# Attention with a routed feed-forward: head values as column tiles, softmax sums over added probability tiles, and reciprocals spread by DMA

## The reference, cut to what matters

```python
def _L0_xattn_ref(q, k, v):              # q = layernorm(x), k = v = ctx; each (4, 512, 512)
    qh, kh, vh = (t.reshape(B, 8, 64, 512) for t in (q, k, v))
    qn, kn = _l2norm(qh, -2), _l2norm(kh, -2)         # over the 64 channels of a head
    sm = softmax(5.0 * einsum('bhdq,bhdk->bhqk', qn, kn), axis=-1)
    return einsum('bhqk,bhdk->bhdq', sm, vh).reshape(B, 512, 512)

x = x + _L0_xattn_ref(_layernorm(x), ctx, ctx)
x = x + _L0_ffn_ref(_layernorm(x), Wg, bg, W1, W2)    # top 2 of 4 experts, 512 tokens each
```

## Time and profile before

| what | us |
|---|---|
| median of 3 runs | 655.43 |
| the profiled execution, its own time | 656.28 |
| span of its trace | 654.3 |
| PE busy | 592.0 (90%) |
| DVE busy | 368.6 (56%) |
| ACT busy | 300.4 (46%) |
| POOL busy | 175.3 (27%) |
| reciprocals L762, mean of one | 3.35 |
| one half-unit's weighted values L1168 (8 records) in the chain | 3.44 to 3.55 |

### The profile page before, as it was taken

The page is one execution under the profiler, slowest core; times in us unless marked ns, Lnnn a source line. Parts: engine busy times, 40 slices in busy tenths (PEclk is TensorE's granted clock), DMA queues, the critical chain, the costliest instruction groups (busy, mean ns, idle before and its releaser), DMA issues.

```text
span 654.3 us, 8188 instructions
## 1 busy us (share of the span) xinstructions
PE 592.0 (90%) x2714; PEld 430.6 (66%) x2714; DVE 368.6 (56%) x638; ACT 300.4 (46%) x454; POOL 175.3 (27%) x139
## 2 busy tenths in 40 slices
PE   1899999999999951299999999999999999999994
PEld 1555555556555541168888888888888888888883
DVE  4678888888888878453425463434734245533312
ACT  2577776777678633044343332434333333434310
POOL 4544445445543600220021051040230120320002
PEclk9999999999999965579999999999999999999998
DMA  4423112221120023133333344151262332451001
GB/s 120 134 79 112 65 64 80 82 94 64 66 95 33 34 81 111 47 87 126 119 105 98 128 145 176 64 189 67 99 221 84 121 116 99 159 190 67 0 1 64
DMA packets 39636, 63.62 MB, mean 97 GB/s; under 512 B 3520, under 2 KB 20032, under 8 KB 39616
## 3 DMA queue, kind: packets, MB, share of 16 engines
q1 hardware_dynamic: 35776, 50.78, 22.7%
q0 software_dynamic: 3840, 12.59, 5.8%
HBM read 50.77 MB, written 12.58 MB: 97 GB/s over the span
## 4 chain that ended last, share of the span: by engine, by line
PE 73%; DVE 15%; issue 4%; POOL 1%; DMA 1%; DVEq 0%; ACT 0%; POOLq 0%
PE two L1299 28%; PE four L1329 9%; PE four L1328 9%; PE four L1326 9%; PE two L1168 9%; DVE p_inv L762 4%; PE four L1158 4%; PE bank_t L1185 1%; DVE o_norm L770 1%; PE bank_t L1137 1%; DVE junk L938 1%; PE bank_m L1145 1%; DVE x_all L772 1%; PE bank_t L1177 1%; DVE ss L723 1%
## 5 line engine op out<-in xcount | busy, mean ns | idle before, releaser
L677 ACT ACTIVATE h_f<-two 128x512 f32<-128x512 f32 x64 | 38.2, 598 | 231.7 <-PE two L1299 231.7
L1168 PE MATMUL two<-prob,v_t 128*128 128x512 f32 x256 | 116.7, 598 | 0.0
L1098 DVE TENSOR_TENSOR h_lo<-h_f,h_hi 128x512 fp32r<-128x512 f32 x64 | 44.1, 689 | 126.1 <-ACT h_hi L678 126.1
L1299 PE MATMUL two<-xt_hi,w_hi 128*128 (+1 forms) x256 | 103.0, 402 | 0.7 <-issue 0.7
L1299 PE MATMUL two<-xt_hi,w_lo 128*128 (+1 forms) x256 | 101.3, 396 | 0.0
L1299 PE MATMUL two<-xt_lo,w_hi 128*128 (+1 forms) x256 | 100.9, 397 | 0.0
L1329 PE MATMUL four<-w_hi,h_lo 128*128 128x512 f32 x256 | 100.5, 393 | 0.0
L1326 PE MATMUL four<-w_hi,h_hi 128*128 128x512 f32 x256 | 100.5, 392 | 0.0
L1328 PE MATMUL four<-w_lo,h_hi 128*128 128x512 f32 x256 | 100.4, 392 | 0.0
L1069 DVE TENSOR_TENSOR w_lo<-raw,w_hi 128x2048 fp32r<-128x2048 f32 x30 | 68.7, 2291 | 23.3 <-ACT w_hi L610 23.3
L582 ACT ACTIVATE prob<-four,rnorm 128x512 f32<-128x512 f32 x128 | 79.5, 695 | 2.3 <-PE four L1158 1.1
(11 more groups left out here) (167 smaller groups left out, 758.2 us busy)
## 6 DMA issues: line engine op xcount, KB each, us to landing
raw<-in_L_ffn_W SPq DMA_DIRECT2D x64, 512.0 KB, 3.9
x_all<-in_x SPq DMA_DIRECT2D x16, 256.0 KB, 2.7
c_sb<-in_ctx SPq DMA_DIRECT2D x16, 256.0 KB, 2.8
out<-x_all SPq DMA_DIRECT2D x16, 256.0 KB, 2.0
x2n_dram<-x2n SPq DMA_DIRECT2D x16, 256.0 KB, 2.1
cst<-in_consts SPq DMA_DIRECT2D x1, 354.5 KB, 4.8
x_got<-x2n_dram,idx_all POOLq DMA_INDIRECT x16
o_got<-out,idx_all POOLq DMA_INDIRECT x16
```

The source lines that it names most:

```text
L677: nc.scalar.activation(h_f[m % 2][:, :], z_ps[m % 2][:, :], ACT.Gelu)
L1098: nc.vector.tensor_tensor(h_lo[m % 2][:, :], h_f[m % 2][:, :], h_hi[m % 2][:, :].bitcast(F32), ALU.subtract).then_inc(h_split, 1)
L1168: last = nc.tensor.matmul(o_ps[h][:, :], v_t[u[1]][:, t, 2 * h:2 * h + 2, :] .rearrange("p a d -> p (a d)"), prob[h][t][:, :], start=(t == ...
L1299: return nc.tensor.matmul(z[:, :], w_part[c][:, w], x_k, start=start, stop=stop)
```

## The change

What it does:

- Values: the values of the two heads lie in one tile of 2 x 64 columns. Each head's matmul has 64 columns and writes its own half of the partitions of one PSUM bank (`o_ps[0]`), as a column tile. The ones leave this operand.
- Sums: probability tiles are added in pairs first (tile 0 + tile 1, tile 2 + tile 3), for head 0 on GpSimd and for head 1 on VectorE. Two matmuls per head with 64 columns of ones make the sums of it, again as column tiles, in `o_ps[1]`.
- Reciprocals: ACT copies the sums out (`take_sums`, one turn later). SP moves the row of each head into `few` (128 x 8), DVE inverts these 8 elements per partition, SP writes them to DRAM, waits, and reads them back broadcast to 64 partitions per head. `residual` waits for that read. For the last two units DVE inverts the full 128 x 512 tile, straight from PSUM.
- Order: on DVE `normalize_x2` of u-2 is now the first thing of a turn and `residual` and `statistics_x2` of u-1 are the last. On POOL the two additions are placed behind waits for `rq_ready` and `xsq_done`, and `key_remainders` moves to the end of the turn, behind a wait for `x2_done`. On PE `values` and `spread_queries` come ahead of the scores. ACT squares the keys and takes the values ahead of the exponentials. `first_low` is cut into 8 pieces of 128 x 512: three of them follow the sums of the last unit, the other five wait for `thr_done` of the router's search rounds, one each.

```diff
+FEW = 2 * D // P
+DVE_HEADS, POOL_HEADS = (1,), (0,)
...
+    inv_dram = nc.dram_tensor("inv_dram", (2 * D,), F32, kind="Internal").ap()
...
-            v_t = [att(f"v_t{n}", [P, TT, 4, DH]) for n in range(2)]
+            v_t = [att(f"v_t{n}", [P, TT, 2, DH]) for n in range(2)]
...
+            half_sum = [[att(f"half_sum{h}{n}", [P, D]) for n in range(2)] for h in range(2)]
+            few = att("few", [P, FEW])
+            few_inv = att("few_inv", [P, FEW])
...
+            def spread_inverse(u):
+
+                n = number(u)
+                sp.wait_ge(sum_taken, n + 1)
+                for h in range(2):
+                    half = slice(h * P // 2, (h + 1) * P // 2)
+                    sp.dma_start(few[half, :], p_sum[DH * h:DH * h + 1, :]).then_inc(few_in, 16)
+                sp.wait_ge(few_done, n + 1)
+                sp.dma_start(inv_dram.rearrange("(p j) -> p j", j=FEW), few_inv[:, :]).then_inc(few_out, 16)
+                sp.wait_ge(few_out, 16 * (n + 1))
+                for h in range(2):
+                    sp.dma_start(p_inv[DH * h:DH * (h + 1), :],
+                                 inv_dram[D * h:D * (h + 1)].rearrange("(a d) -> a d", a=1).broadcast_to([DH, D])
+                                 ).then_inc(inv_in, 16)
...
             load_next((2, 0))
+            spread_inverse((0, 0))
             store_unit((0, 0))
             end = UNITS // 2 - 1
             with sp.Fori(2, end) as h:
                 load_next((h, 1))
+                spread_inverse((h - 2, 1))
                 store_unit((h - 2, 1))
                 load_next((h + 1, 0))
+                spread_inverse((h - 1, 0))
                 store_unit((h - 1, 0))
             load_next((end, 1))
             for u in ((end - 2, 1), (end - 1, 0), (end - 1, 1), (end, 0), (end, 1)):
+                if number(u) < EARLY:
+                    spread_inverse(u)
...
+
+            def half_sums(u, n, h, reused):
+
+                pool.wait_ge(exp_done, TT * number(u) + 2 * n + 2)
+                if reused:
+                    pool.wait_ge(sums_ready, number(u))
+                nc.gpsimd.tensor_tensor(half_sum[h][n][:, :], prob[h][2 * n][:, :], prob[h][2 * n + 1][:, :],
+                                        ALU.add).then_inc(halves_done[h], 1)
...
-            def first_low(c):
+            def first_low(c, q):
 
                 pool.wait_ge(whi_done, c + 1)
-                nc.gpsimd.tensor_tensor(w_lo[c][:, :], raw[c][:, :], w_hi[c][:, :].bitcast(F32), ALU.subtract
-                                        ).then_inc(wlo_done, 1)
+                part = slice(q * HALF // 2, (q + 1) * HALF // 2)
+                low_part = nc.gpsimd.tensor_tensor(w_lo[c][:, part], raw[c][:, part], w_hi[c][:, part].bitcast(F32),
+                                                   ALU.subtract)
+                if q == 3:
+                    low_part.then_inc(wlo_done, 1)
...
             def unit(u, behind, ahead):
-                if not ahead:
-                    pool.wait_ge(x2n_done, number(u) - 1)
-                    for c in range(AHEAD):
-                        first_low(c)
+                n = number(u)
+                for h in POOL_HEADS:
+                    if ahead:
+                        pool.wait_ge(rq_ready, n + 2)
+                    half_sums(u, 0, h, behind > 0)
                 if ahead:
                     if behind:
 
-                        pool.wait_ge(exp_done, TT * number(u))
+                        pool.wait_ge(exp_done, TT * n)
                     key_norms(after(u))
+                for h in POOL_HEADS:
+                    if ahead > 1:
+                        pool.wait_ge(xsq_done, n + 3)
+                    half_sums(u, 1, h, behind > 0)
                 if ahead > 1:
+                    query_norms(after(after(u)))
+                if ahead > 2:
+                    prepare(after(after(after(u))))
+                if ahead > 1:
+                    if behind:
+                        pool.wait_ge(x2_done, n)
                     key_remainders(after(after(u)))
-                    query_norms(after(after(u)))
                 if behind:
                     finish(before(u))
-                if ahead > 2:
-                    prepare(after(after(after(u))))
 
...
+            pool.wait_ge(sums_ready, UNITS)
+            for q in range(3):
+                first_low(0, q)
             finish((UNITS // 2 - 1, 1))
+            for q in range(3, 8):
+                pool.wait_ge(thr_done, q - 1)
+                first_low(q // 4, q % 4)
...
@@ -578,6 +635,8 @@
                 act.wait_ge(scores_ready, g + 1)
                 if reused:
                     act.wait_ge(pv_done, g - TT + 1)
+                    for h in range(2):
+                        act.wait_ge(halves_done[h], 2 * (number(u) - 1) + t // 2 + 1)
...
-                nc.scalar.activation(p_sum[0:DH, :], o_ps[0][DH:P, :], ACT.Copy)
-                nc.scalar.activation(o_sb[0:DH, :], o_ps[0][0:DH, :], ACT.Copy).then_inc(o_taken[0], 1)
-                nc.scalar.activation(p_sum[DH:P, :], o_ps[1][0:DH, :], ACT.Copy).then_inc(sum_taken, 1)
-                nc.scalar.activation(o_sb[DH:P, :], o_ps[1][DH:P, :], ACT.Copy).then_inc(o_taken[1], 1)
+                nc.scalar.activation(o_sb[:, :], o_ps[0][:, :], ACT.Copy).then_inc(o_taken, 1)
+
+            def take_sums(u, reused):
+
+                n = number(u)
+                act.wait_ge(sums_ready, n + 1)
+                if reused:
+                    act.wait_ge(few_in, 32 * n)
+                nc.scalar.activation(p_sum[:, :], o_ps[1][:, :], ACT.Copy).then_inc(sum_taken, 1)
...
             def unit(u, behind, ahead):
+                if behind and ahead:
+                    take_sums(before(u), behind > 1)
+                if ahead:
+                    square_keys(after(u), behind + 1)
+                    take_v(after(u), behind + 1)
                 exponentials(u, 2, behind > 0)
-                if ahead:
-                    take_v(after(u), behind + 1)
                 exponentials(u, 3, behind > 0)
+                if ahead > 1:
+                    square_queries(after(after(u)), True)
                 if behind > 1:
                     take_x2t(before(before(u)))
-                if ahead > 1:
-                    square_queries(after(after(u)), True)
-                    round_keys(after(after(u)), True)
                 if ahead:
                     act.wait_ge(rk_done, number(u) + 2)
                     exponentials(after(u), 0, True)
                     exponentials(after(u), 1, True)
-                if ahead in (1, 2):
-                    split_hi(0, 2 - ahead)
+                if ahead > 1:
+                    round_keys(after(after(u)), True)
+                if not ahead:
+                    for c in range(AHEAD):
+                        split_hi(0, c)
                 take_o(u, behind > 0)
...
+            def invert_few(u):
+
+                n = number(u)
+                dve.wait_ge(few_in, 32 * (n + 1))
+                nc.vector.reciprocal(few_inv[:, :], few[:, :]).then_inc(few_done, 1)
+
             def invert_sums(u):
 
-                n = number(u)
-                dve.wait_ge(sum_taken, n + 1)
-                nc.vector.reciprocal(p_inv[:, :], p_sum[:, :]).then_inc(inv_done, 1)
-
-            def residual(u):
+                dve.wait_ge(sums_ready, number(u) + 1)
+                nc.vector.reciprocal(p_inv[:, :], o_ps[1][:, :]).then_inc(inv_done, 1)
+
+            def half_sums(u, n, h, reused):
+
+                dve.wait_ge(exp_done, TT * number(u) + 2 * n + 2)
+                if reused:
+                    dve.wait_ge(sums_ready, number(u))
+                nc.vector.tensor_tensor(half_sum[h][n][:, :], prob[h][2 * n][:, :], prob[h][2 * n + 1][:, :],
+                                        ALU.add).then_inc(halves_done[h], 1)
+
+            def residual(u, late=0):
 
                 n = number(u)
                 xu = x_all[:, bass.ds(n, 1), :].rearrange("p a d -> p (a d)")
-                dve.wait_ge(o_taken[1], n + 1)
-                dve.wait_ge(inv_done, n + 1)
+                dve.wait_ge(o_taken, n + 1)
+                if late:
+                    dve.wait_ge(inv_done, late)
+                else:
+                    dve.wait_ge(inv_in, 32 * (n + 1))
...
             def unit(u, behind, ahead):
+                if behind > 1:
+                    normalize_x2(before(before(u)), behind > 2)
+                if not ahead:
+                    invert_sums(before(u))
                 if ahead:
                     queries(after(u), after(after(u)) if ahead > 1 else None)
                     sum_key_squares(after(u))
-                if behind:
-                    invert_sums(before(u))
+                for h in DVE_HEADS:
+                    half_sums(u, 0, h, behind > 0)
+                if behind and ahead:
+                    invert_few(before(u))
                 if ahead > 1:
```

(76 more changed lines are left out.)

9 lines of the change are left out of this document (2 added, 7 removed).

## The result

The changed kernel takes 676.55 us (median of 4 runs, 674.61 to 678.20) against 655.33 for the kernel before: a ratio of 1.0325, 95% interval 1.0293 to 1.0357. It is slower by 21.2 us. The forecast was 671, that is 15.5 us slower, in a range from 640 to 690. The profiled execution of the changed kernel took 676.18, span 674.4.

What follows compares the result with a forecast made beforehand. PE bounded the kernel before; after the change a ring of waits would, at 14.4 us a turn against 13.11. Loop +16.8 and last units -1.3 make +15.5: 655.4 + 15.5 = 671 us, range 640 to 690.

Steps and rivals of the forecast that it cites:

- The ring of waits: Attention loop: residual, x2n, SP's queue, DRAM and back to residual; 14.1 us a turn, 13.5 to 15.6.
- the conflict, POOL first: After finish, POOL's addition starts ahead of normalize_x2, so x2n is done at 5.25 rather than 4.25; chance 0.50.
- The sign that I had named: DVE waits for the DMA of p_inv ahead of residual, most of a microsecond or more per turn, or arrives just in time.
- The lock: DVE's instruction stands still while POOL's runs; predicted for x2n beside POOL's addition, about 1.5 us there.
- the first rival: normalize_x2 starts before POOL's addition in the loop: turn 13.3 us, time 653, span 645 to 660; chance 0.32.
- the trip: Reciprocals through DRAM in each loop turn: write 1.5 us, broadcast read 2.4 us, then residual at 14.1.
- The second ring: Loop, from x2n through queries, key norms, POOL's second addition, query norms and widen_queries: 14.2 to 14.5 us a turn.
- the price of two DMA steps: In the loop, the small moves take 1.5 us (1.4 to 2.1), the broadcast read 2.4 (2.0 to 2.7).
- Pairing of column tiles: Two heads' matmuls on PE run side by side: eight value records about 1.75 us; no pairing gives 700, chance 0.07.
- more changes of the array's use: PE switches between whole, row-tiled and column-tiled use perhaps three times more per turn; taken as 0.3 us.
- The last units: From residual of unit 13 to the first key instruction: keys 2.1 us sooner, or 0.4 later; taken as -1.3.
- The rival that PE sets the pace: Rings are short and PE bounds the loop at 11.5 us a turn: time 630; chance 0.11.

Runs made afterwards that it cites:

- e1: Changed kernel plus one GpSimd wait: its first addition of a turn waits until x2n of u-2 is written; 666.43 us, ratio 1.0178.
- e2: Changed kernel with SP issuing the two small moves before waiting for x2n, and VectorE inverting the few elements right after the queries; 666.00 us, ratio 1.0185.
- e5: Changed kernel plus three more pairs of matmuls, overwritten right after, in PE's idle stretch ahead of the weighted values; 678.06 us, ratio 1.0373.
- e3: Changed kernel with the edits of e1 and e2, and GpSimd's query norms placed before its second addition; 652.26 us, ratio 0.9980.
- e6: Changed kernel with the first three pieces of first_low on GpSimd waiting until the early keys are set; 674.33 us, ratio 1.0314.
- e8: Changed kernel with the edits of e3 and e6, and the second additions of both heads on VectorE; 641.60 us, ratio 0.9804 to the kernel before.

## Why the prediction was right

By its own steps, with time 0 at the start of `residual` (119.18 in the profile above):

| step | predicted | measured |
|---|---|---|
| x2 written | 1.52 | 1.53 |
| `k_lo` done | 2.87 | 2.89 |
| L785, now L870, done | 3.05, held up | 2.66, not held up |
| `finish` done | 3.7 | 3.6 |
| x2n done | 5.25, held up | 5.16, held up |
| last move issued | 7.6 | 7.4 |
| `few` landed | 9.1 | 9.7 |
| reciprocals written to SP's wait | 9.5 | 10.0 |
| write landed | 11.0 | 11.4 |
| reads landed, next `residual` | 14.1 | 14.9 |

- *The mechanism held.* The ring of waits through x2n, SP's queue and DRAM sets the turn: e1 and e2 each take one link of it out, and each moves the turn. The forecast of the conflict, POOL first, came true in 12 of 15 units. Of the three others, in two (units 2 and 6) PE, at half rate just before, was late with `rq_ready`, so that POOL's addition came late; in the third (unit 14) POOL had no addition to do there. In e2 and e5, where the granted clock of the loop is 0.98 and 1.00, POOL is first in 14 of 15. The sign that I had named, most of a microsecond of waiting for `p_inv` a turn, came out at about half of one (5.3 us in 160), with as much again for `few`.
- *The lock is nearly half of the loss in the loop.* Without it (e1) the turn is 14.03, not the 13.3 that I gave the first rival, and the time is 666, not 653. So 0.80 of the 1.72 us a turn hung on POOL being first. The rest comes from the trip and the second ring, and the first rival was priced too low by the same DMA steps as the forecast.
- *The second ring* is there too. I put it at 14.2 to 14.5 with the lock; e2 shows 13.85.
- *What was too small* is the price of two DMA steps, and both lay above the high ends that I had given them. The moves took 2.3 us where I took 1.5 (high end 2.1): I had priced them by their few KB and not by what stands ahead of them in the queue, and in e2, with less ahead, they take 1.8. The read took 2.9 for each half, where I took 2.4 (high end 2.7). The write, at 1.4, was close to my 1.5. The whole loop came out 0.44 us a turn over my 14.4, 5.6 us in 13 turns, and the start of the program 1.0 us under, within my 1.5. Together with the last units this is the 20.1 us by which the spans differ, where my sum was 15.5. The Trainium skill, "DMA: Bandwidth & Descriptors", section Anatomy of one DMA, states its fixed cost of about 2.0 us for DMAs issued from GpSimd; those of the trip are issued by SyncE, so my reading of it as a cost of every DMA went too far. By it the ring would have been 15.1 (an estimate), near the 14.91 of this turn; but the write landed in 1.4, well under 2.0, so the agreement is one of the sum and not of each DMA.
- *Pairing of column tiles*: 1.75 us predicted for eight records, 1.77 to 1.94 from start to next start. PE's saving is real, but PE was not on the ring. Where the clock stayed at 1.00 (e3) PE is busy for 11.9 us of a turn (an estimate: 164.84/180 of 12.95), where I had 11.5. The groups of eight records, three a turn and most of them above 1.75, are part of the excess. The 0.3 us that I took for more changes of the array's use stands in no row, before or after.
- *L785*, a 128x1 operation that is L870 after the change, was not held up beside `k_lo`, in no turn. I had argued from a 128x8 operation, and of those one is held up: L785 of the changed kernel takes 1.10 to 1.17 us in four turns of the loop, beside POOL's second addition (at 114.78, 1.11 us), and 0.17 in the others. The reason is open; it cost nothing, since `finish` follows `k_lo` anyway.
- *The last units*: -1.3 predicted; measured -3.8 up to the first key instruction, since the first piece of `first_low` came after x2n and not before it (1.1 us) and the last `residual` came 0.5 us sooner than I had it, and then +2.5, because the pieces met the key instructions (e6). Together -1.3. The agreement is chance in part: I had the right lock and the wrong victim.
- *The rival that PE sets the pace* is out: PE is busy for 87% of the loop and waits in most turns for `x_norm`, which DVE makes soon after x2n. Even with the rings shortened (e8) most turns are 11.8 to 12.6, above the 11.5 that I gave PE.
- *TensorE's clock* was not among my rivals, and I had said only that PE would idle for about 3 us of a turn. It stood idle for 3.45 us at a stretch here, but only for 2.0 us of a mean turn, since at half rate its work took longer, and it fell to half rate in several turns. e5 shows that the time did not hang on it.

## What to carry to other kernels

Busy shares say what an engine could do, not what a turn costs: when work is moved, follow one item once around the ring of in-order queues, DMA queue included, and price each link before counting the busy time saved. An in-order queue passes its first wait on to everything behind it, so put a small, urgent DMA ahead of the wait for a late, lazy one. When GpSimd gets elementwise work, look at what VectorE wants to start within the same few tenths of a microsecond; a single wait that gives VectorE the first go was worth 10 us here.

## What the runs showed of the hardware that was not expected

- Tiny DMAs are not cheap in proportion: 2 KB from SBUF to SBUF took 1.8 us right behind 256 KB of the same queue (e2) and 2.3 right behind 768 KB (the changed kernel), 4 KB to DRAM took 1.4 to 1.7, and 128 KB broadcast from DRAM 2.9, against 2.0 for a store and 2.7 for a load of 256 KB.
- The lock between GpSimd and VectorE met a one-input VectorE copy (`wide_q`, 1.48 for 0.43) and additions with two inputs (L954, 1.46 for 0.38), but not a 128x1 operation (L870, 0.15 us in every turn) that ran within `k_lo`. "SBUF — State Buffer" in the Trainium skill, section Who interferes with whom, names operations in a 2-port mode and those with two SBUF inputs; the first two fit it, and no run here shows why the third was spared.
- TensorE, after 3.45 us without work, worked at 1.2 GHz from 126.45 on (granted clock 0.50; eight records of L1262 in 3.68 us, against 1.94 later), and was back at 2.4 GHz in the middle of a busy stretch, at about 139 (granted clock 0.97 from 139 to 140).
